# An attention and expert block on one core: the joined rounds of attention without products of a constant on TensorE

## The chip, the cores and the metric

The kernel runs on one NeuronCore of a Trainium2 chip. The core has TensorE (PE: matmuls, with weight loads on a queue of their own, PEld), VectorE (DVE), ScalarE (ACT), GpSimd (POOL) and SyncE (SP), which run their own instruction streams and meet only at semaphores. The metric is device time in microseconds, the median of several executions.

## The reference

It is one block on x of 4 x 256 tokens x 256 features, modulated by a condition. Cut to what matters:

```python
mod = (silu(c) @ wmod).reshape(4, 6, 1, -1)
sa, ca, ga, sb, cb, gb = mod[:, 0], ..., mod[:, 5]       # ga, gb: |.| raised to at least 0.25
h = layernorm(x) * (1 + ca) + sa
x = x + ga * attention(h)            # 16 heads of 16, rope, causal softmax, output projection
h = layernorm(x) * (1 + cb) + sb
x = x + gb * experts(h)
# experts: softmax over 64 router logits, the top 8 of each token with their weights renormalised;
# each expert takes at most 128 rows in order of tokens; h = silu(g) * u, then the down projection
```

## The kernel before

**Stages.** Attention works on a batch of 256 tokens at a time (`TPB` = 2 tiles of 128 tokens). The head of the program prepares batch 0. Then come three *joined rounds*, `one_round(it, more)` with `it` = 1, 2, 3. Each finishes batch `it - 1` (softmax and values in `attend`, output projection `o_proj`, second layer norm, `h2_transposes`, `router`, `ranks`) and brings batch `it` as far as its scores' maxima (`split_transposes`, `scores_for_max` in twelve chunks, `neg_transposes`). With `more` true it also projects batch `it + 1` (`front`, `qkv`). Rounds 1 and 2 are one hardware loop with `more` true; the last round is written out with `more` false. Behind it stand `attend` and an epilogue for the last batch, tile by tile, and then 64 experts in a pipeline on all engines.

**What sets the order.** Each engine's instructions run in the order in which its block of the program writes them. There is no scheduler. An engine waits only where its code has `wait_ge` on a semaphore.

**TensorE beside its neighbours in a round.** `scores_for_max` writes chunk n to bank 4 + n % 3 and waits from chunk 3 on until VectorE has reduced chunk n - 3 (`v_max`, L1110). `h2_transposes` waits for VectorE's `hidden_rows` (`v_h2`, last instruction L1158), `router` for ScalarE's copy L616, VectorE's `picks` (from L1164) for the router's result, `ranks` for `picks`. VectorE then reduces chunks 8 to 11 and runs `split_maxima`, whose last instruction L1120 releases `neg_transposes`; ScalarE copies their result (L627), and `attend` waits for this copy. VectorE reads the result of `ranks` in `slots`, written behind `split_maxima`. `slots` gives the positions to which GpSimd scatters the rows, 16 scatters a batch (L518).

**Products of a constant.** `keep_warm(n)` issues n matmuls of the all-ones tile `onesb` with itself, 128 x 128 by 128 x 512 in bf16 (L716), into bank 0, or bank 4 where it is given. Nobody reads the result, and no semaphore is touched. A run issues 105 of them: 33 at the head (13, 6, 10 and 4), 57 in the joined rounds, 8 in the epilogue (4 before each tile's `h2_transposes`) and 7 in front of the experts.

Of the kernel before, what the change touches and what calls it, by code (L numbers as in the profile page):

```python
# [12 lines left out]
def adaln_moe_program(nc, x, wqkvT, bias, woT, routerT, gate_up, down, cond, wmod,  # L13
# [35 lines left out]
    with ctx:  # L49
# [125 lines left out]
        bank = [ctx.enter_context(nc.psum_tensor(f"bank{i}", [P, 512], FP32)) for i in range(8)]  # L175
# [535 lines left out]
        def _(pe):  # L711
            mm = nc.tensor.matmul
            def keep_warm(n, idle=bank[0]):

                for _ in range(n):
                    mm(idle[:, :], onesb, onesb[:, None, :].broadcast_to([P, 4, P]), start=True, stop=True)  # L716
# [23 lines left out]
            def front(it):  # L740

                if not isinstance(it, int) or it > 0:
                    pe.wait_ge(a_kT, 2 * TPB * it)
                pe.wait_ge(v_xn, it + 1)
                for t in range(TPB):
                    for k in range(HC):
                        last = nc.tensor.transpose(bank[3][:, k * S + t * P:k * S + (t + 1) * P],
                                                   xn[:, t, k * P:(k + 1) * P], ident)
                last.then_inc(p_xnT, 1)

            def qkv(it, t, what=(0, 1)):

                pe.wait_ge(a_h1T, HC * (it + 1))
                for n in what:
                    dst, c0, c1 = ((bank[1 + t][:, :], 0, 2 * H), (bank[3][:, t * H:(t + 1) * H], 2 * H, 3 * H))[n]
                    for k in range(HC):
                        mm(dst, h1T[:, k, t * P:(t + 1) * P], wqkv_sb[:, k, c0:c1], start=k == 0, stop=False)  # L757
                    last = mm(dst, ones3, bias3[:, c0:c1], start=False, stop=True)
                if 1 in what:
                    last.then_inc(p_qkv, 1)  # L760

            def split_transposes(it, t):
                pe.wait_ge(v_split, TPB * it + t + 1)
                if t == 1:
                    pe.wait_ge(a_vaug, it + 1)
                for src, bk in ((q_split, (1, 2)[t]), (k_split, (0, 3)[t])):
                    flat = src[:, t, :, :, :].rearrange("p h a c -> p (h a c)")
                    for g in range(NH // 2):
                        last = nc.tensor.transpose(bank16[bk][:, g * P:(g + 1) * P], flat[:, g * P:(g + 1) * P], ident16)
                    last.then_inc(p_qkT, 1)  # L770

            def scores_for_max(it, n0, n1, b):

                for n in range(n0, n1):
                    g, i0, nh, qt = chunks[n]
                    if n in (0, 4):
                        pe.wait_ge(v_qT, TPB * it + qt + 1)
                        pe.wait_ge(a_kT, 2 * (TPB * it + qt + 1))
                    heads = groups[g][i0:i0 + nh]
                    bk = bank[4 + n % 3]  # L780
                    if n >= 3:
                        pe.wait_ge(v_max, 12 * it + n - 2)
                    elif b is None and n == 2:
                        pe.wait_ge(a_mod, 2)
                    w = (qt + 1) * P
                    view = bk[:, 0:len(heads) * w].rearrange("p (h k) -> p h k", k=w)
                    mm(view[:, :, w - P:w], identb, maskb[:, None, :].broadcast_to([P, len(heads), P]),
                       start=True, stop=False, skip_group_check=True)
                    for i, h in enumerate(heads):
                        last = mm(view[:, i, :], qT[:, h // 2, qt * P:(qt + 1) * P], kz[:, h, 0:w],  # L790
                                  start=False, stop=i == len(heads) - 1, skip_group_check=True)
                    last.then_inc(p_s1, 1)

            def neg_transposes(it):
                pe.wait_ge(v_neg, it + 1)
                for t in range(TPB):
                    last = nc.tensor.transpose(bankb[0][:, t * P:(t + 1) * P],
                                               neg2[:, t, :, :].rearrange("p c h -> p (c h)"), identb)
                last.then_inc(p_negT, 1)
# [41 lines left out]
            def att_transposes(b):  # L841

                pe.wait_ge(a_att, 2 * b + 2)
                for t in range(TPB):
                    for g in range(4):
                        last = nc.tensor.transpose(bank[4 + t][:, g * P:(g + 1) * P],
                                                   att_sb[:, g // 2, (g % 2) * S + t * P:(g % 2) * S + (t + 1) * P], ident)
                    last.then_inc(p_attq, 1)

            def out_transposes(b, ts, alt):  # L850
                for t in ts:
                    pe.wait_ge(v_att, TPB * b + t + 1)
                    for k in range(HC):
                        last = nc.tensor.transpose(back_bank("attT", alt)[:, k * S + t * P:k * S + (t + 1) * P],
                                                   att_tok[:, t, k * P:(k + 1) * P], ident)
                last.then_inc(p_attT, 1)

            def o_proj(ts, n, alt):
                pe.wait_ge(a_attT, n)
                for t in ts:  # L860
                    dst = back_bank("o", alt)[:, t * H:(t + 1) * H]
                    for k in range(HC):
                        mm(dst, attT[:, k, t * P:(t + 1) * P], wo_sb[:, k, :], start=k == 0, stop=False)
                    last = mm(dst, ones3, bias3[:, 3 * H:4 * H], start=False, stop=True)
                last.then_inc(p_o, 1)

            def h2_transposes(ts, n, alt):
                pe.wait_ge(v_h2, n)
                for t in ts:
                    for k in range(HC):  # L870
                        last = nc.tensor.transpose(back_bank("h2T", alt)[:, k * S + t * P:k * S + (t + 1) * P],
                                                   rows[:, t, k * P:(k + 1) * P], ident)
                last.then_inc(p_h2T, 1)

            def router(ts, n, alt):

                pe.wait_ge(a_h2T, n)
                for t in ts:
                    for k in range(HC):
                        last = mm(back_bank("router", alt)[:, t * E:(t + 1) * E], h2T[:, k, t * P:(t + 1) * P],  # L880
                                  router_sb[:, k, :], start=k == 0, stop=k == HC - 1)
                last.then_inc(p_log, 1)

            def ranks(ts, n, alt):

                pe.wait_ge(v_sel, n)
                for t in ts:
                    dst = back_bank("router", alt)[:, 256 + t * E:256 + (t + 1) * E]
                    mm(dst, prefixb, sel[:, t, :], start=True, stop=False)
                    last = mm(dst, onesb, seen[:, t, :], start=False, stop=True)  # L890
                last.then_inc(p_cum, 1)

            def one_round(it, more):
                b = it - 1
                attend(b)
                split_transposes(it, 0)
                att_transposes(b)
                split_transposes(it, 1)
                out_transposes(b, ALL, 0)
                scores_for_max(it, 0, 2, b)  # L900
                o_proj(ALL, it, 0)
                scores_for_max(it, 2, 5, b)
                if more:
                    front(it + 1)
                    keep_warm(4)
                    qkv(it + 1, 0)
                else:
                    keep_warm(12)
                scores_for_max(it, 5, 7, b)
                keep_warm(2)  # L910
                h2_transposes(ALL, it, 0)
                scores_for_max(it, 7, 8, b)
                router(ALL, it, 0)
                scores_for_max(it, 8, 11, b)
                if more:
                    qkv(it + 1, 1, (0,))
                else:
                    keep_warm(6)
                ranks(ALL, it, 0)
                scores_for_max(it, 11, 12, b)  # L920
                if more:
                    qkv(it + 1, 1, (1,))
                keep_warm(4 if more else 8)
                neg_transposes(it)
                keep_warm(3, bank[4])

            front(0)
            keep_warm(10)
# [466 lines left out]
```

## Time and profile before

| | |
|---|---|
| median of 3 runs | 353.6 us (352.01 to 356.23) |
| profiled execution, its own time | 353.68 us |
| span of its instructions | 351.8 us |
| mean granted TensorE clock over the span | 0.901 |
| TensorE busy | 266.4 us (76%) |
| VectorE, ScalarE, GpSimd busy | 208.5, 141.5, 176.4 us |
| joined rounds, start of one `attend` to the next | 45.63, 79.62, 114.17, 149.51 us |
| last scatter issued; first product before the experts | 197.76; 200.00 us |

How to read it: the busy time of an engine is summed over all stages, and the rounds make up about a third of the span. A granted clock of 1.00 stands for 2.4 GHz and 0.50 for 1.2 GHz. Matmuls overlap in the pipeline of TensorE, so the time from one start to the next, not the duration of one, tells what a matmul costs.

### The profile page before, as it was taken

How to read it: one execution, taken by the hardware profiler on the slowest of the kernel's cores; microseconds unless marked ns; L12 is line 12 of the kernel's file. 1: busy time of each engine (PE TensorE's matmuls, PEld its weight loads, DVE VectorE, ACT ScalarE, POOL GpSimd, SP SyncE). 2: the span in 40 equal slices, each digit the busy share in tenths (PEclk: the TensorE clock that was granted, in tenths of full speed). 3: DMA queues.
4: the chain of work that ended last, by engine and by line, in shares of the span. 5: the costliest groups of instructions: out<-in, count | busy, mean ns of one | idle time of the engine just before them, and what ended most of it. 6: DMA issues, size and time to landing. Idle time of an engine off the chain costs nothing.

```text
span 351.8 us, 6793 instructions
## 1 busy us (share of the span) xinstructions
PE 266.4 (76%) x1825; PEld 181.8 (52%) x1825; DVE 208.5 (59%) x602; ACT 141.5 (40%) x408; POOL 176.4 (50%) x167
## 2 busy tenths in 40 slices
PE   8697999999999987996240297979888998994000
PEld 4235467557655764574120176757666877772000
DVE  3657987798679848813550044655655665664086
ACT  3118078218711870163120055546545565551000
POOL 4700000004545346456657517878888888888400
PEclk9899999999999999899855599999999899998555
DMA  4960399999999722212219599999999999866993
GB/s 139 359 209 3 122 306 335 349 387 281 285 306 277 194 78 78 76 47 91 105 61 263 171 259 284 226 200 254 199 238 203 206 159 143 134 75 68 215 314 120
DMA packets 67550, 68.76 MB, mean 195 GB/s; under 512 B 5490, under 2 KB 64167, under 8 KB 67529
## 3 DMA queue, kind: packets, MB, share of 16 engines
q1 hardware_dynamic: 55240, 52.09, 51.0%
q0 software_dynamic: 12288, 16.42, 25.4%
q8 instruction: 10, 0.16, 0.2%
q14 instruction: 12, 0.09, 0.1%
HBM read 37.77 MB, written 31.21 MB: 196 GB/s over the span
## 4 chain that ended last, share of the span: by engine, by line
PE 38%; DMA 19%; issue 16%; DVE 12%; ACT 8%; POOL 4%; another core or an unknown queue 1%; DVEq 1%; SPq 1%; POOLq 0%; ACTq 0%
DMA sum<-stage 16%; PE bank L757 6%; PE bank L716 6%; POOL slot_rows L518 3%; ACT kz L601 3%; PE bank L817 3%; PE bank L833 3%; PE bank L831 2%; DVE arena L1323 2%; PE bank L984 2%; PE bank L790 2%; DMA arena<-sum 2%; PE bank L828 2%; DVE stage L1307 2%; ACT arena L582 2%
## 5 line engine op out<-in xcount | busy, mean ns | idle before, releaser
L535 POOL DMA_INDIRECT sum<-stage x64 | 98.8, 1543 | 30.5 <-DVE stage L1307 15.5
L518 POOL DMA_INDIRECT slot_rows<-stage x48 | 48.1, 1002 | 33.9 <-issue 12.7
L1307 DVE TENSOR_SCALAR stage<-bank,stage 128x256 f32<-128x256 f32 x64 | 34.8, 543 | 40.5 <-DMA sum<-stage 33.8
L984 PE MATMUL bank<-arena,stage 128*128 (+1 forms) x256 | 53.8, 333 | 0.2 <-ACT stage L682 0.2
L716 PE MATMUL bank<-onesb 128*128 128x512 bf16 x105 | 32.2, 450 | 17.7 <-DMA slot_rows<-rows,slot_idx 16.6
L998 PE MATMUL bank<-arena,stage 96*128 (+1 forms) x128 | 42.0, 410 | 0.6 <-DVE stage L1307 0.6
L984 PEld LDWEIGHTS bank<-arena,stage 128*128 128x128 f32 x256 | 40.9, 193 | 1.0 <-ACT stage L682 0.4
L682 ACT ACTIVATE stage<-bank 128x256 f32<-128x256 f32 x64 | 24.5, 384 | 41.7 <-PE bank L975 32.1
L506 POOL COPY stage<-slot_idx 128x16 uint32<-128x16 uint32 x3 | 0.6, 198 | 71.4 <-DMA sum<-zero_row 63.3
L1110 DVE TENSOR_REDUCE rmax<-bank 128x2 f32<-128x512 f32 (+1 forms) x48 | 30.2, 683 | 3.6 <-PE bank L790 2.3
L992 PE MATMUL bank<-cst,stage 128*96 128x128 f32 x64 | 18.9, 295 | 13.3 <-DVE stage L1298 11.3
L582 ACT ACTIVATE arena<-bank 128x512 f32<-128x512 f32 x48 | 26.3, 598 | 5.1 <-PE bank L833 4.3
L716 PEld LDWEIGHTS bank<-onesb 128*128 128x128 bf16 x105 | 11.2, 113 | 31.1 <-issue 24.7
L689 ACT ACTIVATE stage<-bank 128x96 f32<-128x96 f32 x64 | 16.1, 251 | 24.8 <-PE bank L984 10.4
L975 PE MATMUL bank<-cst,stage 128*128 128x128 f32 x128 | 25.1, 279 | 0.0
L757 PE MATMUL bank<-arena 128*128 128x512 f32 (+1 forms) x64 | 24.3, 502 | 0.8 <-ACT arena L565 0.8
L833 PE MATMUL bank<-stage 128*128 128x256 bf16 (+1 forms) x128 | 24.6, 246 | 0.0
L831 PE MATMUL bank<-arena,kz 128*128 128x256 f16 (+1 forms) x128 | 24.6, 246 | 0.0
L1289 DVE COPY stage<-stage 128x3 f32<-128x3 f32 x64 | 13.1, 205 | 17.9 <-DMA stage<-slot_rows 17.4
L1297 DVE SCALAR_TENSOR_TENSOR stage<-stage,bank 128x96 f32<-128x96 f32 x64 | 16.6, 259 | 10.3 <-ACT stage L692 8.6
L975 PEld LDWEIGHTS bank<-cst,stage 128*128 128x128 f32 x128 | 18.3, 146 | 7.3 <-issue 1.5
L998 PEld LDWEIGHTS bank<-arena,stage 96*128 96x128 f32 x128 | 19.4, 191 | 4.9 <-ACT stage L699 1.0
(142 smaller groups left out, 468.9 us busy)
## 6 DMA issues: line engine op xcount, KB each, us to landing
slot_rows<-zero_row SPq DMA_DIRECT2D x8, 1040.0 KB, 13.3
stage<-slot_rows SPq DMA_DIRECT2D x64, 130.0 KB
arena<-in_gate_up SPq DMA_DIRECT2D x10, 768.0 KB
sum<-zero_row SPq DMA_DIRECT2D x4, 1152.0 KB, 12.4
arena<-in_gate_up SPq DMA_DIRECT2D x24, 192.0 KB
arena<-sum SPq DMA_DIRECT2D x16, 256.0 KB, 6.1
arena<-in_down SPq DMA_DIRECT2D x5, 768.0 KB
arena<-in_down SPq DMA_DIRECT2D x12, 192.0 KB
```

The lines of the kernel that those rows point to most:

```text
L518: pool.indirect_dma_start(slot_rows, bass.IndirectOffsetOnAxis(ap=idx[:, t, k:k + 1], axis=0), src[:, t, :], None, bounds_check=SLOTS - 1, ...
L535: pool.indirect_dma_start(sums[a], bass.IndirectOffsetOnAxis(ap=meta[:, j, 2:3].bitcast(U32), axis=0), ye[:, j % NACC, :], None, bounds_ch ...
L582: nc.scalar.activation(dst, bank[4 + n % 3][:, :], ACT.Exp, scale=SCALE).then_inc(a_exp, 1)
L716: mm(idle[:, :], onesb, onesb[:, None, :].broadcast_to([P, 4, P]), start=True, stop=True)
L757: mm(dst, h1T[:, k, t * P:(t + 1) * P], wqkv_sb[:, k, c0:c1], start=k == 0, stop=False)
L831: mm(view[:, i, :], kz[:, h, kt * P:(kt + 1) * P], qT[:, h // 2, kt * P:S], start=False, stop=False, skip_group_check=True)
L833: last = mm(view[:, i, :], pickb[:, h, :], negT[:, kt * P:S], start=False, stop=i == len(heads) - 1, skip_group_check=True)
L975: last = nc.tensor.transpose(bank[j % 2][:, k * CAP:(k + 1) * CAP], xe[:, j, k * P:(k + 1) * P], ident)
L984: last = mm(bank[2 + q % 2][:, 0:GU + 1], xeT[:, q % 2, k * CAP:(k + 1) * CAP], expert_w[:, s - 1, k * (GU + 1):(k + 1) * (GU + 1)], start ...
L998: mm(bank[6 + q % 2][:, 0:H], hidT[:, q % 2, :], expert_w[0:I, s - 3, HC * (GU + 1):EW], start=True, stop=True).then_inc(p_ye, 1)
L1110: V.tensor_reduce(rmax[:, qt, h0:h0 + 2 * nh - 1:2], src, AX.X, ALU.max).then_inc(v_max, 1)
L1307: V.tensor_scalar(ye[:, q % NACC, :], bank[6 + q % 2][:, 0:H], gatew[:, q:q + 1], meta[:, q, 1:2], ALU.mult, ALU.mult).then_inc(v_ye, 1)
```

## The change

The six calls of `keep_warm` inside `one_round` of TensorE's block are deleted: 4, 2, 4 and 3 products in a round with `more`, 12, 2, 6, 8 and 3 in the last one. The products at the head, in the epilogue and before the experts stay.

```diff
--- before.py
+++ after.py
@@ -902,27 +902,19 @@
                 scores_for_max(it, 2, 5, b)
                 if more:
                     front(it + 1)
-                    keep_warm(4)
                     qkv(it + 1, 0)
-                else:
-                    keep_warm(12)
                 scores_for_max(it, 5, 7, b)
-                keep_warm(2)
                 h2_transposes(ALL, it, 0)
                 scores_for_max(it, 7, 8, b)
                 router(ALL, it, 0)
                 scores_for_max(it, 8, 11, b)
                 if more:
                     qkv(it + 1, 1, (0,))
-                else:
-                    keep_warm(6)
                 ranks(ALL, it, 0)
                 scores_for_max(it, 11, 12, b)
                 if more:
                     qkv(it + 1, 1, (1,))
-                keep_warm(4 if more else 8)
                 neg_transposes(it)
-                keep_warm(3, bank[4])
 
             front(0)
             keep_warm(10)
```

On TensorE, at the end of a round of the loop, from the value projection of the next batch (L757, L758) over `neg_transposes` (L797) to the first score of `attend` (L828):

```order
 L757 MATMUL bank<-arena 128x256 x2
 L758 MATMUL bank<-stage 128x256
-L716 MATMUL bank<-onesb 128x512 x4
 L797 MATMUL bank<-stage 128x128 x2
-L716 MATMUL bank<-onesb 128x512 x3
-L947 REGISTER_ALU
-L947 COMPARE_AND_BRANCH
+L939 REGISTER_ALU
+L939 COMPARE_AND_BRANCH
 L828 MATMUL bank<-stage 128x2x128
 L831 MATMUL bank<-arena,kz 128x256
```

The transposes and the first scores now follow directly on the projection, each behind its own wait; the loop's own register instructions only change their line.

In the last round on TensorE, from chunk 4 of the scores (L787 and L790) to chunk 7 behind `h2_transposes` (L871), before the change:

```order
L787 MATMUL bank5<-stage 128x2x128
L790 MATMUL bank5<-kz,arena 128x256 x2
L716 MATMUL bank0<-onesb 128x512 x12
L787 MATMUL bank6<-stage 128x2x128
L790 MATMUL bank6<-kz,arena 128x256 x2
L787 MATMUL bank4<-stage 128x2x128
L790 MATMUL bank4<-kz,arena 128x256 x2
L716 MATMUL bank0<-onesb 128x512 x2
L871 MATMUL bank0<-cst,rows 128x128 x4
L787 MATMUL bank5<-stage 128x2x128
```

and after it:

```order
L787 MATMUL bank5<-stage 128x2x128
L790 MATMUL bank5<-kz,arena 128x256 x2
L787 MATMUL bank6<-stage 128x2x128
L790 MATMUL bank6<-kz,arena 128x256 x2
L787 MATMUL bank4<-stage 128x2x128
L790 MATMUL bank4<-kz,arena 128x256 x2
L871 MATMUL bank0<-cst,rows 128x128 x4
L787 MATMUL bank5<-stage 128x2x128
```

Chunks 4, 5 and 6 and the transposes are neighbours now, with nothing between them. Further on in the same round, from chunk 11 over `neg_transposes` to `attend`:

```order
 L787 MATMUL bank<-stage 128x2x128
 L790 MATMUL bank<-kz,arena 128x256 x2
-L716 MATMUL bank<-onesb 128x512 x8
 L797 MATMUL bank<-stage 128x128 x2
-L716 MATMUL bank<-onesb 128x512 x3
 L828 MATMUL bank<-stage 128x2x128
 L831 MATMUL bank<-arena,kz 128x256
```

Eleven products go there; no other instruction of TensorE changes its place, and the other engines' orders are untouched.

## Rows read from the trace of the kernel before

**Rows 1.** Page, part 4: the chain that ended last, shares of the span by line

```profile
DMA sum<-stage 16%; PE bank L757 6%; PE bank L716 6%; POOL slot_rows L518 3%; ACT kz L601 3%; PE bank L817 3%; PE bank L833 3%; PE bank L831 2%; DVE arena L1323 2%; PE bank L984 2%; PE bank L790 2%; DMA arena<-sum 2%; PE bank L828 2%; DVE stage L1307 2%; ACT arena L582 2%
```

**Rows 2.** Timeline, TensorE, first joined round: start, us, operation, count, idle before

```profile
64.87 1.03 PE L716 MATMUL bank<-onesb 128*128 128x512 bf16 x4
66.29 1.98 PE L757 MATMUL bank<-arena 128*128 128x512 f32 x4 [0.40 <-ACT arena L565]
...
70.96 0.66 PE L871 MATMUL bank<-cst,rows 128*128 128x128 f32 x4
...
72.30 1.10 PE L880 MATMUL bank<-router_sb,arena 128*128 128x64 f32 x8 [0.24 <-ACT arena L616]
...
78.86 0.28 PE L797 MATMUL bank<-stage 128*128 128x128 bf16 x2
...
79.62 0.28 PE L828 MATMUL bank<-stage 128*128 128x256 bf16 x1
```

**Rows 3.** Timeline, VectorE, first joined round

```profile
70.22 0.69 DVE L1158 TENSOR_TENSOR rows<-arena 128x512 f32<-128x512 f32 x1
...
78.60 0.19 DVE L1120 TENSOR_TENSOR stage<-stage 128x32 bf16<-128x32 f32 x1
```

**Rows 4.** Timeline, ScalarE, first joined round

```profile
79.17 0.39 ACT L627 ACTIVATE stage<-bank 128x256 bf16<-128x256 bf16 x1 [4.00 <-PE bank L797]
```

**Rows 5.** Timeline, TensorE, last joined round

```profile
134.23 2.75 PE L716 MATMUL bank<-onesb 128*128 128x512 bf16 x12
136.82 0.28 PE L787 MATMUL bank<-stage 128*128 128x256 bf16 x1
...
140.22 0.66 PE L871 MATMUL bank<-cst,rows 128*128 128x128 f32 x4 [1.87 <-DVE rows L1158]
...
141.57 1.44 PE L880 MATMUL bank<-router_sb,arena 128*128 128x64 f32 x8 [0.24 <-ACT arena L616]
...
148.74 0.28 PE L797 MATMUL bank<-stage 128*128 128x128 bf16 x2
```

**Rows 6.** Timeline, VectorE, last joined round

```profile
136.08 1.28 DVE L1110 TENSOR_REDUCE rmax<-bank 128x4 f32<-128x512 f32 x2
...
139.48 0.69 DVE L1158 TENSOR_TENSOR rows<-arena 128x512 f32<-128x512 f32 x1
...
148.49 0.19 DVE L1120 TENSOR_TENSOR stage<-stage 128x32 bf16<-128x32 f32 x1
```

**Rows 7.** Windows: us; busy of PE, PEld, DVE, ACT, POOL; granted clock; DMA; GB/s

```profile
44.80:134.20 89.40, 85.50 (x806) 57.47 (x806) 69.15 (x167) 50.57 (x95) 25.56 (x32) 1.00 0.94 275
149.50:160.80 11.30, 10.62 (x141) 7.77 (x140) 1.09 (x7) 7.29 (x13) 5.85 (x9) 1.00 0.14 49
```

**Rows 8.** Timeline, GpSimd: the first scatter of the last batch

```profile
178.55 0.97 POOL L518 DMA_INDIRECT slot_rows<-rows,slot_idx  x1 [3.85 <-DVE slot_idx L1196]
```

**Rows 9.** Chain of waits in order of time, epilogue and the landing behind it

```profile
171.21 3.24 another core or an unknown queue
...
197.76 2.02 DMA slot_rows<-rows,slot_idx
```

**Rows 10.** Source line 716 within the joined rounds: ns min/median/max, first and last start

```profile
L716 PE MATMUL bank<-onesb x57: 379/379/634, 64.9 to 149.3; 128*128 128x512 bf16 x57
```

**Rows 11.** Windows (columns as in rows 7) around the low clock, last round

```profile
142.00:143.00 1.00, 1.00 (x8) 0.96 (x7) 0.56 (x1) 0.00 (x0) 0.83 (x1) 0.59 0.01 0
145.00:146.00 1.00, 1.00 (x4) 0.36 (x3) 0.97 (x3) 0.00 (x0) 0.07 (x1) 0.70 0.37 133
```

**Rows 12.** Timeline, TensorE, epilogue: transposes and router products at both clocks

```profile
169.58 0.44 PE L871 MATMUL bank<-cst,rows 128*128 128x128 f32 x2 [1.18 <-DVE rows L1158]
170.65 0.66 PE L880 MATMUL bank<-router_sb,arena 128*128 128x64 f32 x4 [0.63 <-issue]
...
179.57 0.69 PE L871 MATMUL bank<-cst,rows 128*128 128x128 f32 x2 [1.70 <-DVE rows L1158]
180.73 1.11 PE L880 MATMUL bank<-router_sb,arena 128*128 128x64 f32 x4 [0.47 <-ACT arena L616]
```

## The prediction

> **What bounds the kernel now.** I read the chain of waits first. It names the constant products (L716) with 6% of the span [rows 1]. That is a trap: the chain follows the instruction before on the same engine wherever that engine was never idle, so filler in front of a wait is counted as if it were needed. So I went to the order of time on TensorE around each group of products in the joined rounds, and for each asked what ended last: the products, or the signal that the next instruction waits for.
>
> In the first joined round [rows 2] the four products behind `front` are followed by a wait of 0.40 us for ScalarE. The two in front of `h2_transposes` end as VectorE ends L1158 at 70.91 (70.22 + 0.69) [rows 3]; the transposes start at 70.96. The four in front of `neg_transposes` end as VectorE ends L1120 at 78.79 [rows 3]; the transposes start at 78.86. The three behind it lie beside ScalarE's copy L627, which ends at 79.56 [rows 4]; attention starts at 79.62. The second round reads alike. In the last round [rows 5, 6]: twelve products before chunk 5, whose bank is free when the first reduction of the pair at 136.08 ends (half of 1.28 us, so at 136.72; start 136.82); two before the transposes at 140.22, which still waited 1.87 us for L1158; six before `ranks`, whose result VectorE reads only after L1120; eight before `neg_transposes`, held by L1120, which ends at 148.68 (start 148.74); three beside the copy. So in these rounds VectorE sets the pace around every group, and TensorE inside attention, where it is busy 10.62 of 11.30 us against 7.29 of ScalarE [rows 7].
>
> Behind the last round nothing absorbs a delay. Attention of the last batch, the epilogue's tokens 0 and their slots come before the last 16 scatters; GpSimd has stood idle for 3.85 us, waiting for the slots, when it starts the first of these at 178.55 [rows 8], and the experts wait for the landing of the sixteenth, 197.76 plus 2.02 us [rows 9].
>
> **What the change removes.** 57 products go: 13 in each of two rounds, 31 in the last [rows 10]. Back to back they start every 0.216 us (twelve take the 2.59 us from 134.23 to 136.82 [rows 5]), so they fill 57 x 0.216 = 12.3 us of TensorE. That is the upper bound of any gain, were all on the path. By the readings above every group is covered, so I take 0 for the direct gain; the starts stand 0.05 to 0.10 us behind their signals, which leaves nothing to win.
>
> **What it costs: the clock.** The granted clock is 1.00 over the whole stretch from 44.8 to 134.2 [rows 7]: TensorE ran at 2.4 GHz. It fell to 0.50 (1.2 GHz) at about 142.2, and rose at about 145.6 (0.59 and 0.70 as means of the two microseconds in which it switched [rows 11]), though TensorE was fully busy in both of them. What went before: the wait of 1.87 us that ends at 140.22, then short transposes and 64-column products. So a thin stretch much shorter than a full stop brought the clock down, even with the products in place, and it stayed down for 3.4 us of full work.
>
> After the change the last round has three more thin places. Where 2.6 us of products stand before chunk 5, TensorE idles; before the transposes the idle time grows from 1.9 to 2.3 us; before `ranks` and `neg_transposes` another 1.3 and 1.7 us are empty (6 and 8 products), and 0.65 us (3) before attention. I expect the clock low from before 140 at the latest, and low again, or still, when attention of the last batch starts. Three terms:
>
> 1. The serial TensorE pieces before VectorE's picks. Half clock prices stand in the epilogue [rows 12]: two transposes 0.44 us at full clock, 0.69 at half; four router products 0.66 and 1.11. So two transposes cost 0.25 us more and four 0.5; four router products cost 0.45 more and eight 0.9, which makes 2.0 us of the 1.10 that they took in the first round at full clock [rows 2], against 1.44 here, where the clock fell in the middle [rows 5]: 0.56 more. VectorE waits for the router's result before its picks, so 0.5 + 0.56 = 1.1 us passes through (bounds 0, if the clock holds until 142, and 1.1). The score chunks at half clock stay behind VectorE's reductions: 0.
> 2. `neg_transposes` at half clock: two transposes of half the data width, so between 0 and the 0.25 us of the pair above; 0.1.
> 3. Attention of the last batch. Each microsecond at half clock costs 0.5 us there, since TensorE is its bound. The only low stretch under full work that I have is 3.4 us [rows 11]. Attention can meet the rest of one (2 us) or, since its beginning is half filled with idle time, all of two (6.8 us). I take 4 us, nearest to the one row: 2.0 us, bounds 1.0 and 3.4.
>
> Sum: 0 + 1.1 + 0.1 + 2.0 = 3.2 us. The profiled execution took 353.68 us with a span of 351.8; the median of the three runs is 353.6, so the two agree, and the forecast is 353.6 + 3.2 = 356.8 us.
>
> In the two earlier rounds the new idle times are 1.3 us behind `front`, 0.4 before the transposes, and 0.8 and 0.65 around `neg_transposes`, with matrix work of full width between. That is thinner than before but denser than the stretch that made the clock fall, so 0 there.
>
> For the row that fell I looked at what the notes say. The Trainium skill, "TensorE: Matmul & The Clock Gate", section "Why this matters for your kernels", advises against long idle gaps between bursts of products, because an idle stretch sends the clock back to half. A reader who takes only a long unbroken stop as the cause would add nothing for terms 1 to 3 and get 353.6. The trace's fall behind 1.87 us of idle time speaks for the stricter reading.
>
> **The rivals.**
> - The clock holds, or falls and rises early enough: no stop in the new order is longer than 2.6 us, and the fall in the profile may be a matter of luck in time that differs between executions (the three runs spread from 352.01 to 356.23). Then only part of term 1 is left: 353.6 to 355. Against it: the last round now has thin places in a row, not one.
> - The clock falls in the earlier rounds too, at the idle times around `neg_transposes`. Each fall then lies in front of a dense attention stage and costs 3.4 / 2 = 1.7 us: 356.8 + 1.7 to 356.8 + 3.4 = 358.5 to 360.2. For it: two groups of idle time stand close together there, right behind 64-column products. Against it: the value projection lies between.
> - On the other side, not slower: the unexplained gap. In the epilogue the chain shows 3.24 us put to "another core or an unknown queue" at 171.21 [rows 9], between the end of the router's products for tokens 0 and VectorE's copy. Nothing in the program accounts for it. If it is tied to where TensorE's instructions lie or to the moment they are reached (44 products of the code go), it can shrink or vanish. It decides from the point where it gives back more than the 3.2 us: 353.6 + 3.2 - 3.24 = 353.6, and 350.4 if the clock also holds. For it: only one of the two passes through this code shows it. Against it: I see no cause.
> - The change not doing what it says is excluded: the order of instructions shows every group gone and nothing else moved.
>
> **How the numbers follow.** Forecast as summed (355.2 to 358.2, term 3 at its bounds and the rest of the scatter with term 1): 0.50. Clock holds or matters little: 0.23. Falls in the earlier rounds too: 0.16. The gap goes: 0.11. The range runs from 352.6 to 360.0 (the lower end takes in the spread of runs below the median): it leaves out the case with a vanished gap and a held clock below, and two falls in earlier rounds with the upper bound of term 3 above. About 1% (3.5 us) is what a measurement of this kernel can tell from no change. Slower by more than that needs 357.1: some two fifths of the likeliest case and all of the second rival, 0.36. Faster by more than 1% (below 350.1) needs both parts of the gap case: 0.04. Within 1%: 0.60.
>
> **What would show it.** In the changed kernel's windows of the last round the granted clock should be 0.50 for most of 138 to 152 and for some 4 us behind the start of attention; the router's eight products should take about 2.0 us, the stage of attention 13 us for 11.3. In the first two joined rounds `h2_transposes`, `neg_transposes` and attention should start at the same distance from VectorE's and ScalarE's ends as now, with idle time named after L1158, L1120 and L627 and the clock at 1.00. If the first scatter of the last batch comes at the same distance from the end of attention, the epilogue passed the delay on. I am wrong if those starts move ahead, if the clock stays at 1.00 in the last round, or if the 3.24 us gap is gone.

## The result, and the profile after

The changed kernel takes 356.67 us (median of 22 runs, 354.01 to 359.41), the kernel before 354.8 us in the same comparison (22 runs, 350.49 to 357.11). The ratio is 1.007, with a 95% interval of 1.0048 to 1.0092: slower by 1.7 to 3.3 us, and no gain anywhere. The profiled execution of the changed kernel took 358.21 us (span 356.4, mean granted clock 0.872), that of before 353.68 (351.8, 0.901). This pair differs by 4.5 us, more than the medians do, so it gives the places and not the size.

**First joined round, TensorE** (start in us, duration, instruction, count, idle time before it and what ended that), which answers to [rows 2]:

```profile
66.34 1.98 PE L757 MATMUL bank<-arena 128*128 128x512 f32 x4 [1.26 <-ACT arena L565]
...
71.02 0.66 PE L871 MATMUL bank<-cst,rows 128*128 128x128 f32 x4 [0.34 <-DVE rows L1150]
...
78.90 0.28 PE L797 MATMUL bank<-stage 128*128 128x128 bf16 x2 [0.79 <-DVE stage L1112]
```

VectorE's and ScalarE's lines behind the change are eight lower than before (L1150 was L1158, L1112 was L1120, L1102 was L1110). Where products stood, there is now idle time with the name of the signal behind it, and the instruction behind it starts where it did: 66.34 against 66.29, 71.02 against 70.96, 78.90 against 78.86.

**Windows** of the changed kernel: the two rounds of the loop, the last third of the last round, attention of the last batch in two parts, and a piece of the epilogue. Columns as in [rows 7].

```profile
44.80:134.20 89.40, 80.34 (x779) 55.23 (x780) 69.06 (x168) 50.34 (x95) 26.23 (x32) 1.00 0.94 276
139.00:149.50 10.50, 6.86 (x31) 4.64 (x31) 8.75 (x24) 1.27 (x5) 5.73 (x6) 0.50 0.19 66
150.50:155.80 5.30, 5.30 (x29) 3.82 (x30) 1.01 (x6) 2.39 (x4) 1.97 (x5) 0.51 0.07 25
155.80:164.10 8.30, 7.59 (x113) 5.29 (x111) 0.00 (x0) 5.05 (x9) 4.01 (x5) 1.00 0.14 50
166.10:176.30 10.20, 9.25 (x26) 5.20 (x27) 5.12 (x17) 1.17 (x4) 5.92 (x7) 0.51 0.18 65
```

Read the busy time and the clock together. In the loop TensorE is busy for 80.34 us instead of 85.50 [rows 7] and keeps its 2.4 GHz. In the last round it is at 1.2 GHz from 138.6 us on, for the whole last third, and the third window is the costly one: TensorE is busy for all of its 5.30 us, at half clock, inside attention.

**Last round and last attention, TensorE**, which answers to [rows 5]:

```profile
136.95 0.28 PE L787 MATMUL bank<-stage 128*128 128x256 bf16 x1 [2.42 <-DVE rmax L1102]
...
140.35 1.12 PE L871 MATMUL bank<-cst,rows 128*128 128x128 f32 x4 [2.31 <-DVE rows L1150]
...
142.15 1.97 PE L880 MATMUL bank<-router_sb,arena 128*128 128x64 f32 x8
...
149.62 0.40 PE L797 MATMUL bank<-stage 128*128 128x128 bf16 x2 [1.78 <-issue]
...
150.49 0.39 PE L828 MATMUL bank<-stage 128*128 128x256 bf16 x1 [0.48 <-ACT stage L627]
...
163.47 0.86 PE L817 MATMUL bank<-arena 128*32 128x256 f32 x16 [0.71 <-ACT arena L582]
```

The router's eight products take 1.97 us; they took 1.44 before and 1.10 in the first round. Attention of the last batch starts 0.98 us later than before, 0.11 of it brought along from earlier rounds. From its first scores (L828) to the start of the last of its products with the values (L817, at 164.06, in the group that begins at 163.47) it takes 13.57 us; before, the same two starts were 11.02 us apart.

**Epilogue, TensorE**, which answers to [rows 12]:

```profile
166.11 1.97 PE L846 MATMUL bank<-cst,arena 128*128 128x128 f32 x8 [1.78 <-ACT arena L589]
...
169.19 2.07 PE L863 MATMUL bank<-arena 128*128 128x256 f32 x4 [0.47 <-ACT arena L606]
...
172.68 2.07 PE L863 MATMUL bank<-arena 128*128 128x256 f32 x4 [0.47 <-ACT arena L606]
...
177.28 0.66 PE L880 MATMUL bank<-router_sb,arena 128*128 128x64 f32 x4 [0.47 <-issue]
```

The clock fell again at 165.9, which it did not do there before (L846 1.09 us for the same eight, L863 1.13 for the same four). From the last values (164.06) to the end of the slots of tokens 0 it takes 17.08 us. Before it took 17.16, but 3.24 of these were the unexplained gap [rows 9], which is gone. So the low clock cost about 3.2 us here (17.08 against the 13.92 that are left without the gap), and the vanished gap gave the same back.

**GpSimd**, first and last scatter of the last batch, which answers to [rows 8]:

```profile
182.00 0.97 POOL L518 DMA_INDIRECT slot_rows<-rows,slot_idx  x1 [0.95 <-issue]
...
201.19 0.98 POOL L518 DMA_INDIRECT slot_rows<-rows,slot_idx  x1 [0.30 <-issue]
```

Both are 3.4 us later than before (178.55 and 197.76). As a sum: 0.11 from the loop, 0.87 in the last round, 2.55 in the last attention, -0.08 in the epilogue, together 3.45. The experts add 1.15 to the span's difference; from the last scatter to the end the profiles of all kernels here take 153.2 to 155.5 us, so this lies within their scatter.

### The profile page after: what moved, and what is told of

Read it like the earlier page. It is cut to its first block, busy times and chain, and to the rows that moved or that the text cites. A ratio compares the mean times of both kernels' runs of the same rounds, so it can differ in the third digit from the quotient of the medians.

```text
span 356.4 us, 6679 instructions
## 1 busy us (share of the span) xinstructions
PE 262.7 (74%) x1768; PEld 181.1 (51%) x1768; DVE 208.2 (58%) x602; ACT 141.2 (40%) x408; POOL 177.3 (50%) x167
## 4 chain that ended last, share of the span: by engine, by line
PE 32%; DMA 22%; DVE 17%; issue 14%; ACT 7%; POOL 6%; SPq 1%; DVEq 1%; POOLq 0%; ACTq 0%
DMA sum<-stage 18%; POOL slot_rows L518 4%; PE bank L757 4%; PE bank L817 3%; PE bank L833 3%; PE bank L831 2%; PE bank L863 2%; DMA arena<-sum 2%; DVE arena L1315 2%; PE bank L716 2%; DVE stage L1299 2%; ACT arena L582 2%; PE bank L828 2%; DVE rmax L1102 2%; POOL sum L535 2%
## 5 line engine op out<-in xcount | busy, mean ns | idle before, releaser
L1102 DVE TENSOR_REDUCE rmax<-bank 128x2 f32<-128x512 f32 (+1 forms) x48 | 30.2, 683 | 3.6 <-PE bank L790 2.3
L716 PE MATMUL bank<-onesb 128*128 128x512 bf16 x48 | 17.5, 528 | 17.7 <-DMA slot_rows<-rows,slot_idx 16.6
L831 PE MATMUL bank<-arena,kz 128*128 128x256 f16 (+1 forms) x128 | 26.2, 257 | 0.0
L757 PE MATMUL bank<-arena 128*128 128x512 f32 (+1 forms) x64 | 24.3, 502 | 2.5 <-ACT arena L565 2.5
L833 PE MATMUL bank<-stage 128*128 128x256 bf16 (+1 forms) x128 | 26.1, 257 | 0.0
L699 ACT ACTIVATE stage<-bank 96x128 f32<-96x128 f32 x64 | 17.3, 270 | 6.1 <-PE bank L984 3.7
```

The costliest lines, as they stand in the source:

```text
L831: mm(view[:, i, :], kz[:, h, kt * P:(kt + 1) * P], qT[:, h // 2, kt * P:S], start=False, stop=False, skip_group_check=True)
L833: last = mm(view[:, i, :], pickb[:, h, :], negT[:, kt * P:S], start=False, stop=i == len(heads) - 1, skip_group_check=True)
L1102: V.tensor_reduce(rmax[:, qt, h0:h0 + 2 * nh - 1:2], src, AX.X, ALU.max).then_inc(v_max, 1)
```

## The experiments

The runs came in three sets. The kernel before takes 354.47 us (median) beside the first four, 349.02 beside the next four and 349.28 beside the last three. So ratios are compared, and stages only within a set. "The first chips" are those of the result and of experiments 1 to 4, where the last attention takes 11.0 us at full clock; "the others" are those of experiments 5 to 11, where it takes 10.24. Edits are shown against the kernel before.

**1. Only the loop's products go.**

```diff
-                    keep_warm(4)
                     qkv(it + 1, 0)
...
-                keep_warm(2)
+                keep_warm(0 if more else 2)
...
-                keep_warm(4 if more else 8)
+                keep_warm(0 if more else 8)
                 neg_transposes(it)
-                keep_warm(3, bank[4])
+                keep_warm(0 if more else 3, bank[4])
```

> Only the products in the two rounds of the loop are gone (13 each); the last round keeps its 31. Theory (the cost lies in the last round and in the attention behind it): the granted clock stays at 1.00 from 16 to 134 us, every start in the loop's rounds stands where it was, ratio to before 0.997 to 1.003. Rival (falls in the loop's rounds too): at least one stretch at 0.50 between 60 and 134 us, 1.7 us lost for each, ratio 1.005 or more.

Measured: 354.43 us, ratio 1.0008 (0.9968 to 1.0047). The windows of the loop and of the last attention:

```profile
44.80:134.20 89.40, 80.25 (x779) 55.15 (x779) 68.97 (x168) 50.55 (x95) 25.01 (x32) 1.00 0.94 275
149.70:160.90 11.20, 10.39 (x141) 7.76 (x140) 1.09 (x7) 7.17 (x13) 5.83 (x9) 1.00 0.14 49
```

The loop's 26 products neither cost nor hold anything. The last attention takes 11.14 us, at full clock, as before. This profile also has the gap of the epilogue, even longer than before, between the router's products and VectorE's copy of their result (VectorE idle for 4.16 us, 3.9 of them behind the end of the products):

```profile
175.71 0.22 DVE L1163 COPY stage<-bank 128x64 f32<-128x64 f32 x1 [4.16 <-remote]
```

**2. Only the last round's 31 go.** The other half of the change: `keep_warm(2 if more else 0)`, `keep_warm(4 if more else 0)`, `keep_warm(3 if more else 0, bank[4])`, and the two `else` branches gone.

> Only the 31 products of the last joined round are gone; the loop's rounds keep theirs. Theory: all of the change's cost, +2 to +3 us, ratio 1.005 to 1.010; clock 0.50 from 137 to 140 us until at least 152; the router's eight products take 1.9 to 2.0 us, the last attention starts some 0.9 us later and lasts 2 to 3 us longer than at full clock. Rival (loop's rounds share the cost): less than half of that, ratio below 1.004.

Measured: 356.85 us, ratio 1.009 (1.0062 to 1.0118). The clock is low from 136.2 to 153.3, in two windows here, and attention takes 12.48 us (1.46 more than 11.02):

```profile
136.20:150.40 14.20, 8.71 (x39) 5.38 (x39) 12.18 (x34) 2.06 (x8) 7.39 (x8) 0.50 0.21 76
150.50:153.30 2.80, 2.80 (x14) 1.90 (x15) 0.97 (x6) 1.09 (x2) 0.98 (x4) 0.50 0.00 0
```

With experiment 1 this places the whole cost of the change in the last round. The gap of the epilogue isn't there, though none of the loop's products was touched.

**3. All 57 stay, but 64 columns wide instead of 512.** This parts the number of instructions from the work of TensorE.

```diff
+            def keep_narrow(n, idle=bank[0]):
+
+                for _ in range(n):
+                    mm(idle[:, 0:64], onesb, onesb[:, 0:64], start=True, stop=True)
```

> All 57 products of the joined rounds stay in number and place, but each is 64 columns wide instead of 512, so the code keeps its instructions and TensorE is nearly as idle as without them. Theory (activity of TensorE and the clock): as the changed kernel, ratio 1.004 to 1.010, clock 0.50 from before 140 us into the last attention. Rival (the number and place of the instructions, the gap of 3.24 us with them): as before, ratio 0.997 to 1.003, with the clock as before.

Measured: 357.38 us, ratio 1.0101 (1.0058 to 1.0144): as slow as without them. The twelve of the last round take half a microsecond:

```profile
135.68 0.51 PE L721 MATMUL bank<-onesb 128*128 128x64 bf16 x12
```

The clock is low from 141.3 to 148.1 and from 151.5 to 154.9, so for 3.2 us inside the last attention, which takes 12.67 us (+1.65). What the products do for the clock, they do by the time that they keep TensorE at work, not by standing between the instructions.

**4. Of the 57 only the last eleven stay** (8 in front of `neg_transposes` of the last round, 3 behind it). If the attention is what costs, these are the ones nearest to it.

```diff
-                keep_warm(4 if more else 8)
+                keep_warm(0 if more else 8)
                 neg_transposes(it)
-                keep_warm(3, bank[4])
+                keep_warm(0 if more else 3, bank[4])
```

(and all the others gone)

> Of the joined rounds' products only the last eleven stay: the 8 in front of the last neg_transposes and the 3 behind it. Theory A (the low clock is a cost only where attention meets it, and the eleven raise it in time): the router's delay of 0.9 us remains, attention runs mostly at 1.00, +0.9 to +1.2 us, ratio 1.003. Theory B (filler that starts at half clock takes 0.43 us each, 3.4 us for eight, and so ends after the signal it was to hide behind): neg_transposes start 1.0 to 1.5 us later than in the changed kernel, which eats most of what the earlier rise of the clock gives; +2 to +3 us, ratio 1.005 to 1.009.

Measured: 356.56 us, ratio 1.0069 (1.003 to 1.0107). TensorE and, below, VectorE:

```profile
146.28 3.62 PE L716 MATMUL bank<-onesb 128*128 128x512 bf16 x8
149.69 0.42 PE L797 MATMUL bank<-stage 128*128 128x128 bf16 x2
149.90 1.24 PE L716 MATMUL bank<-onesb 128*128 128x512 bf16 x3
150.98 0.27 PE L828 MATMUL bank<-stage 128*128 128x256 bf16 x1
```

```profile
148.01 0.19 DVE L1114 TENSOR_TENSOR stage<-stage 128x32 bf16<-128x32 f32 x1
```

The attention runs at full clock again and takes 11.05 us; that part of the loss is gone. But the eight products were started at half clock (low from 137.0 to 150.7) and take 3.62 us where 1.9 were meant, so VectorE's signal of 148.2 finds TensorE busy until 149.69. From the first attention to the last it takes 106.76 us, against 104.79 in the changed kernel and 103.88 before. A filler that is hidden at 2.4 GHz is late at 1.2: what it gives to the clock it takes from the path. By this run the eleven pay only where the clock is still high when they come.

**5. Of the 57 only the last round's first fourteen stay** (12 before chunk 5 and 2 before `h2_transposes`).

```diff
-                    keep_warm(6)
...
-                keep_warm(4 if more else 8)
                 neg_transposes(it)
-                keep_warm(3, bank[4])
```

(and the loop's gone as in 1)

> Of the joined rounds' products only the first fourteen of the last round stay (12 in front of chunk 5, 2 in front of h2_transposes); the 6, 8 and 3 behind are gone, and those of the loop. Theory (thin places in a row; attention of the last batch pays for a low clock at its start): transposes and router run as before (first fall no earlier than 142 us), but the clock is at 0.50 again or still when the last attention starts, which lasts 1.5 to 3 us longer: ratio 1.004 to 1.008. Rival (the head of the last round decides, since it is there that the clock first falls): as before, 0.997 to 1.003.

Measured: 350.79 us beside 349.02, ratio 1.0056 (1.0024 to 1.0088). Around the beginning of attention at 147.99:

```profile
138.20:147.90 9.70, 6.90 (x33) 4.39 (x31) 7.97 (x24) 1.62 (x6) 4.47 (x5) 0.50 0.20 70
148.00:151.90 3.90, 3.90 (x22) 2.89 (x23) 1.01 (x6) 1.47 (x3) 1.96 (x5) 0.50 0.00 0
```

The clock falls at 138.2, right behind the wait of 1.87 us in front of the transposes (they start at 138.00), which these fourteen leave as it was. Without the seventeen behind it the clock doesn't come back before attention does the lifting itself: 12.12 us instead of 10.24 on this chip (+1.88).

**6. Nine products instead of two in that wait.** If thin work brings the clock down, filling the one wait that was left open in the kernel before should hold it, and beat that kernel.

```diff
-                keep_warm(2)
+                keep_warm(2 if more else 9)
```

> As the kernel before, with 9 instead of 2 products in front of the last round's h2_transposes, which fills the wait of 1.87 us there (7 x 0.216 = 1.5 us). Theory: the clock no longer falls at 142 us, the router's eight products take 1.10 instead of 1.44 us, the last attention starts 0.3 to 0.4 us earlier, and executions in which the old fall reached further gain more: ratio 0.994 to 1.000. Rival (the fall comes from the transposes and the 64-column router products, not from the wait): the clock falls at the same place and the ratio is 1.000 or above.

Measured: 347.44 us, ratio 0.9954 (0.9922 to 0.9985). TensorE in the last round, and a window over it:

```profile
135.84 2.11 PE L716 MATMUL bank<-onesb 128*128 128x512 bf16 x9
138.31 0.66 PE L871 MATMUL bank<-cst,rows 128*128 128x128 f32 x4 [0.36 <-DVE rows L1158]
...
139.65 1.10 PE L880 MATMUL bank<-router_sb,arena 128*128 128x64 f32 x8 [0.24 <-ACT arena L616]
```

```profile
130.00:148.00 18.00, 16.49 (x104) 9.24 (x105) 15.67 (x44) 2.67 (x10) 9.74 (x10) 1.00 0.21 75
```

The clock stays at 1.00 from 17 to 167 us, the transposes still wait for VectorE (0.36 us), so the seven more are hidden, and the router is back at 1.10 us. From the first attention to the last it takes 101.30 us, against 102.99 in run 8.

**7. The same idea in the epilogue**: 3, 2, 2 and 8 products in its waits and 9 and 14 instead of 4 before the transposes.

```diff
+            keep_warm(3)
...
+                keep_warm(2)
...
-                keep_warm(4)
+                keep_warm(9 if t == 0 else 14, bank[4])
...
+                keep_warm(2, bank[4])
...
+                if t == 0:
+                    keep_warm(8, bank[4])
```

> As the kernel before, with further products in the epilogue's waits: 3 in front of att_transposes, 2 in front of each o_proj and each router, 9 and 14 instead of 4 in front of the two h2_transposes, 8 behind the router of tokens 0. Theory (the epilogue is serial and pays for a low clock, and the gap of some 3 us behind the router of tokens 0 comes with TensorE going idle there): clock 1.00 up to 184 us, the gap gone, first scatter of the last batch 2 to 4 us earlier, ratio 0.990 to 0.996. Rival A (the gap is not tied to TensorE's activity): the gap stays, ratio 0.997 to 1.001. Rival B (filler ends behind the signals): slower, above 1.002.

Measured: 349.12 us, ratio 1.0007 (0.9974 to 1.0039): nothing. The 0.990 to 0.996 that I expected counted on the gap, and run 8 shows that on this chip the kernel before has none to give back. The clock was low in the last round, from 140.8 to 147.7, where its wait was left open; then it was held to 181.8 us. But from the last values to the slots of tokens 0 it took 14.15 us, against 14.14 in run 8, where the clock also held up to the first tile's router products.

**8. The kernel before once more, with a profile** (on the chip of 5 to 7; no edit).

> The kernel before once more, for a second profile. If the gap behind the router of tokens 0 belongs to this kernel it is there again with 3 to 4 us, and the clock falls once between 139 and 146 us for some 3.4 us or not at all, and stays at 1.00 through the last attention. If the gap is a chance of one execution it is missing.

Measured: 348.21 us. The clock falls at 138.7 and rises at 145.6, attention takes 10.24 us, and there is no gap. The router's eight products take 1.97 us here, in the kernel before itself:

```profile
138.20 0.67 PE L871 MATMUL bank<-cst,rows 128*128 128x128 f32 x4 [1.87 <-DVE rows L1158]
...
139.56 1.97 PE L880 MATMUL bank<-router_sb,arena 128*128 128x64 f32 x8
```

TensorE in the epilogue and, below, VectorE, which starts its copy right behind the products:

```profile
168.80 0.66 PE L880 MATMUL bank<-router_sb,arena 128*128 128x64 f32 x4 [0.47 <-ACT arena L616]
```

```profile
169.50 0.23 DVE L1164 COPY stage<-bank 128x64 f32<-128x64 f32 x1
```

So the fall of the clock belongs to the kernel before (two profiles of two), while the gap is in one profile of two. Without the gap the last scatter of GpSimd's third batch (start 172.02) ends as the first of the last batch may begin (about 173). So gains in the epilogue alone have GpSimd next behind them.

**9. Six, without the loop's products**: the best of both, 1 and 6 together.

```diff
-                    keep_warm(4)
...
-                keep_warm(2)
+                keep_warm(0 if more else 9)
...
-                keep_warm(4 if more else 8)
+                keep_warm(0 if more else 8)
                 neg_transposes(it)
-                keep_warm(3, bank[4])
+                keep_warm(0 if more else 3, bank[4])
```

> In the last round 12, 9, 6, 8 and 3 products (9 instead of 2 in front of h2_transposes), and none in the loop's two rounds. Theory (the loop's products do nothing, those of the last round carry the clock to the last attention): as with the 9 and the loop's products in place, ratio 0.992 to 0.999, clock 1.00 from the head to the epilogue. Rival (the loop's products matter on a chip or at a time where thin places fall badly): a low stretch of 3.4 us in one of the loop's rounds in the profile, ratio above 1.000.

Measured: 346.81 us, ratio 0.9936 (0.9908 to 0.9964). It is faster than the kernel before and, as an estimate from ratios of two sets, 1.3% faster than the changed one (0.9936 / 1.007 = 0.987). The last round and the last attention:

```profile
132.00:145.40 13.40, 11.89 (x73) 6.22 (x70) 12.53 (x37) 2.05 (x8) 8.03 (x8) 1.00 0.25 88
145.40:155.80 10.40, 10.40 (x142) 7.76 (x140) 1.17 (x7) 7.41 (x14) 5.85 (x9) 1.00 0.15 53
```

From the first attention to the last: 101.32 us, the same as in 6.

**10. Nine, with fifty more products before the experts**, issued while TensorE waits 16.6 us for the last scatters, so that its seven before the experts find the full clock.

```diff
+            keep_warm(50)
```

> As the one before, and 50 more products between the last slots and the landing of the last scatter, where TensorE stands idle for some 15 us, so that the 7 in front of the experts run at full clock (0.216 instead of 0.43 us each) and end before the first expert's rows are loaded. Theory (the experts' start waits for the 7 products at half clock, 3.15 us, 0.9 us longer than for the rows): first expert 0.8 to 1.0 us earlier against the last scatter, ratio 0.001 to 0.004 below the one before. Rival A (the experts' pace is set by the adding DMAs, which absorbs an earlier start): the first transposes come earlier, the time is the same. Rival B (50 products at a clock that stays low last 21 us and delay the experts by some 6 us): ratio above 1.01.

Measured: 347.28 us, ratio 0.9936 (0.9902 to 0.997), as 9. The seven of this kernel, and below those of 9:

```profile
191.46 1.69 PE L716 MATMUL bank<-onesb 128*128 128x512 bf16 x7 [1.58 <-DMA slot_rows<-rows,slot_idx]
```

```profile
192.13 3.10 PE L716 MATMUL bank<-onesb 128*128 128x512 bf16 x7 [16.64 <-DMA slot_rows<-rows,slot_idx]
```

The first transposes of the experts, again of this kernel and below of 9:

```profile
193.65 0.77 PE L975 MATMUL bank<-cst,stage 128*128 128x128 f32 x4 [0.51 <-DMA stage<-slot_rows]
```

```profile
195.06 0.60 PE L974 MATMUL bank<-cst,stage 128*128 128x128 f32 x4
```

The seven take 1.69 instead of 3.10 us, and TensorE's first transposes of the experts come 0.83 us earlier behind the start of the last scatter (4.35 against 5.18). But from the last scatter to the end it is 153.48 us, against 153.17 in 9: none of the 0.83 us arrives. That the experts are paced by the DMAs that add the rows up fits this and the chain, but it is not shown. This profile has one more difference from that of 9, a stretch of low clock inside the experts in which TensorE is busy throughout, and by itself that could have eaten the 0.83 us:

```profile
208.70:212.10 3.40, 3.40 (x12) 2.90 (x12) 1.67 (x6) 1.09 (x5) 2.87 (x2) 0.50 1.16 292
```

The median, 347.28 against 346.81 us, shows no gain either.

**11. The changed kernel once more, with a profile** (on the chip of 9 and 10).

> The changed kernel once more, for a second profile: clock low from 136 to 140 us until some microseconds into the last attention, which lasts 1 to 3.4 us longer than the 10.2 to 11 of full clock, half of the low time in it; router's eight products 1.9 to 2.0 us. The gap behind the router of tokens 0 was there in both profiles of the first chips with the last round's products and in none since; if it is bound to the chip and not to the kernel, it is missing here too.

Measured: 350.87 us beside a median of 349.28. The clock is low from 135.6 to 152.6, 4.2 us of it in attention, which takes 12.29 us (+2.05 on 10.24); there is no gap.

```profile
138.28 1.11 PE L871 MATMUL bank<-cst,rows 128*128 128x128 f32 x4 [2.05 <-DVE rows L1150]
...
140.08 1.97 PE L880 MATMUL bank<-router_sb,arena 128*128 128x64 f32 x8
...
148.42 0.40 PE L828 MATMUL bank<-stage 128*128 128x256 bf16 x1 [0.48 <-ACT stage L627]
```

Beside run 8, the second profile of the kernel before, the router takes the same 1.97 us, and from the first attention to the last it is 102.74 us against 102.99: in this pair the round itself costs nothing, and attention is the whole loss. (The two are from different chips, on both of which attention takes 10.24 us at full clock.)

## Why the prediction was right

Forecast 356.8 us, from 353.6 + 3.2. Measured 356.67, or, with the ratio, 0.7% of 354 = 2.5 us. That the two times meet to 0.1 us is luck: the three runs from which the forecast starts have a median 1.2 us below that of the 22, and the added 3.2 us are 1.3 more than the medians' difference (1.9) and 0.7 more than the ratio gives. By its steps:

**Direct gain 0: right.** In each group of the loop idle time with the expected name took the place of the products, and the next instruction starts 0.04 to 0.06 us later than before. Experiment 1 gives 1.0008. The chain's 6% for L716 [rows 1] was no path; the changed kernel has waits in the same places.

**Loop rounds hold their clock: right**, in every profile; without the products TensorE is busy for 80.25 (experiment 1) to 80.34 of 89.40 us. The rival with falls there is out.

**Terms 1 and 2, 1.2 us in the last round: 0.3 too large in one pair of profiles, all of it in the other.** In the first pair the router took 1.97 us (2.0 forecast) and the transposes 1.12, but the last attention starts only 0.87 us later for what the round itself adds. Part of the 0.5 us for the transposes doesn't reach VectorE's last signal; which part I didn't separate. In the second pair (runs 8 and 11) the last attention comes 0.25 us earlier, counted from the first, than in the kernel before. The term leaned on the one place at which the clock had fallen in the kernel before, 142.2 us, in the middle of the router; in its second profile it fell at 138.7 and had already cost the router its 0.87 us.

**Term 3, 2.0 us: right, as a mechanism and nearly in size.** Seven pairs of a low stretch inside the last attention and a lengthening:

| kernel | low inside, us | longer by, us |
|---|---|---|
| after | 5.2 | 2.55 |
| after, second profile | 4.2 | 2.05 |
| 5, fourteen kept | 3.9 | 1.88 |
| 3, narrow | 3.2 | 1.65 |
| 2, last round's gone | 2.8 | 1.46 |
| 1, loop's gone | 0 | 0.12 |
| 4, last eleven kept | 0 | 0.03 |

Each microsecond at half clock costs 0.5 us, as the prediction took it; my 4 us of low clock were 5.2 and 4.2 us in the changed kernel's two profiles, so that 2.0 stands for 2.55 and 2.05, and 2.8 to 3.9 us in experiments 2, 3 and 5.

**The rivals.** "The clock holds" is out: it fell in both profiles of the changed kernel, at 138.6 and 135.6 us. The one row of before (a fall behind 1.87 us of idle time) was a better guide than a reading of the Trainium skill, "TensorE: Matmul & The Clock Gate", section "Why this matters for your kernels", that goes by its advice against long idle gaps alone: the longest stop of the changed kernel's last round is 2.42 us in both profiles, and that of experiment 5, in front of its transposes, 1.87 us. Filling that very wait held the clock (experiment 6).

**"The gap goes" came true in the profile; what it hangs on is not shown.** It is in the first profile of before and in that of experiment 1, and in none of the eleven others, the second one of before among them. On the first chips these two are the kernels that keep all of the last round's products at full width, and the four that don't (after, experiments 2, 3 and 4) are without the gap; on the other chips none of seven has it, with the products or without. So the products alone don't bring it; whether the chips, the order or both together do, no run parts. In the first pair of profiles its absence gave 3.2 us back.

**What was missing: the epilogue's clock.** My sum ended with the last attention. In the changed kernel's profile the clock fell again at 165.9 us and cost some 3.2 us before the slots, which the vanished gap hid. That the sum of stages (3.45 us) stands so near to my 3.2 is luck in that respect. The medians leave it little room on average: the last round and the attention make 0.87 + 2.55 = 3.4 us in the first pair of profiles and -0.25 + 2.05 = 1.8 us in the second, against 1.7 to 3.3 measured. It is no single case: in the first profile of the changed kernel and in those of experiments 2, 3 and 4 the clock falls 13.4 to 16.9 us behind the start of the last attention, in those of before (both), of 1, 5, 6, 9 and 10 and in the second one of the changed kernel only after 20.1 us or more. But all four early falls are on the first chips, and there the time from the last values to the slots of tokens 0 comes out alike in every profile, 17.1 to 18.1 us, with the gap or with the early fall; on the others it is 13.8 to 14.3 us in all seven, whatever the kernel. So this stage differs between the chips, and not clearly by the change.

**What stays open.** The releaser of the gap, why the clock falls early in the epilogue of one profile of the changed kernel and not of the other, and whether either belongs to the first chips.

## What to carry to other kernels

A product of a constant that ends before the signal behind it costs nothing and gains nothing by itself; its worth is the clock of the dense stage that comes next, so judge it by the granted clock there, and, where TensorE bounds that stage as it does here, by 0.5 us for each microsecond at 1.2 GHz. Such products have to be complete: here a stretch with most waits filled and one of 1.87 us left open lost the clock, and seven more products in that wait gained 0.5%, while the ones in front of the signal, run at half clock, made it late. Where the work around the waits is dense of itself, as in the loop, they can go.

## What the runs showed of the hardware

- The clock fell without a long stop: in the kernel before at 142.2 and, second profile, 138.7 us, 2.0 and 0.5 us behind a wait of 1.87 us; in the changed kernel with no stop over 2.42 us; in experiment 5 at 138.2 us, right behind a wait of 1.87 us.
- It kept 1.00 through the loop with waits of up to 1.26 us where products of full width lie between.
- A stretch of low clock had no fixed length: around the last round 3.4 us (before), 6.8 (before, second profile), 13.7 (experiments 4 and 5) and 17.1 (after, both profiles, and experiment 2).
- The same last attention takes 11.0 to 11.1 us at full clock on the first chips and 10.24 on the others, and the kernel before 354.5 and 349.0 us: more than the change is worth, so only ratios within a set compare. From the last values to the slots of tokens 0 it is 17.1 to 18.1 us in six profiles on the first chips and 13.8 to 14.3 in seven on the others.
- VectorE's copy behind the first router products of the epilogue started 3.2 us (before) and 3.9 us (experiment 1) after their end in two profiles, with a releaser that the profile calls remote, and at once in all the others.
